# Linear attention on one Trainium2 core: the sums of the log decays made by a VectorE scan and spread by transfers, in place of TensorE products

## What is computed

```
q, k = elu(x @ Wq) + 1, elu(x @ Wk) + 1;  v = x @ Wv
a = sigmoid(x @ Wa + ba + 2.0)                    # one decay per token and head
S = a_t * S + k_t v_t^T;  z = a_t * z + k_t       # a recurrence over the tokens
out_t = (q_t S) / (q_t z + eps)
x1 = layernorm(x + out @ Wo)
```

## Time and profile before

| | us |
|---|---|
| three runs | 1453.0, 1449.99, 1451.87; median 1451.87 |
| the profiled execution, its own time | 1452.94 |
| its span, first to last instruction | 1450.9 |
| TensorE busy over the span | 1315.6 (91%) |
| ScalarE, VectorE, GpSimd busy over the span | 953.5, 833.1, 745.7 |
| the stage of the change | from the start to about 745 |

### The profile page before, as it was taken

The page is one execution under the profiler, slowest core; times in us unless marked ns, Lnnn a source line. Parts: engine busy times, 40 slices in busy tenths (PEclk is TensorE's granted clock), DMA queues, the critical chain, the costliest instruction groups (busy, mean ns, idle before and its releaser), DMA issues. The chain is left out here.

```text
span 1450.9 us, 31123 instructions
## 1 busy us (share of the span) xinstructions
PE 1315.6 (91%) x10437; PEld 1115.7 (77%) x10437; DVE 833.1 (57%) x1707; ACT 953.5 (66%) x2168; POOL 745.7 (51%) x841
## 2 busy tenths in 40 slices
PE   5899999999999999999988999982599999999780
PEld 4788888888888888888876777761488888888680
DVE  3345554445454455544556888857366666666564
ACT  4577767777777777777745777772466666656553
POOL 2244443444444444443547777740357777776753
PEclk9999999999999999999999999995599999999895
DMA  3300100001000100010023343422346666666737
GB/s 138 82 9 30 31 23 25 21 23 31 23 31 16 30 24 30 24 37 9 23 80 86 107 104 98 112 83 72 113 136 153 153 155 154 155 157 163 180 78 239
DMA packets 136851, 117.54 MB, mean 81 GB/s; under 512 B 46578, under 2 KB 121690, under 8 KB 136730
## 3 DMA queue, kind: packets, MB, share of 16 engines
q1 hardware_dynamic: 121754, 95.36, 21.6%
q0 software_dynamic: 14976, 20.62, 8.1%
HBM read 79.89 MB, written 33.58 MB: 78 GB/s over the span
## 5 line engine op out<-in xcount | busy, mean ns | idle before, releaser
L345 POOL TENSOR_SCALAR_AFFINE_SELECT a_decay<-a_decay 128x256 f32<-128x256 f32 x256 | 115.2, 454 | 258.2 <-ACT a_decay L433 256.7
L565 DVE TENSOR_TENSOR a_probs<-a_ps_s,a_decay 128x384 f32<-128x384 f32 x256 | 131.6, 552 | 158.5 <-PE a_ps_o L752 147.4
L354 POOL TENSOR_TENSOR a_key_sum<-a_probs 128x256 f32<-128x256 f32 x128 | 94.5, 738 | 169.9 <-DVE a_probs L565 157.9
L1877 POOL DMA_INDIRECT sum_rows<-e_y_out,e_target x78 | 125.8, 1613 | 81.0 <-ACT e_y_out L1931 56.5
L396 ACT ACTIVATE a_qk_exp<-a_ps_qk 128x512 f32<-128x512 f32 x128 | 76.5, 598 | 137.2 <-PE a_ps_qk L658 130.0
L658 PE MATMUL a_ps_qk<-a_xT_hi,a_w_hi 128*128 128x256 f32 x512 | 144.8, 283 | 3.6 <-ACT a_qk_relu L397 3.6
L658 PE MATMUL a_ps_qk<-a_xT_hi,a_w_lo 128*128 128x256 f32 x512 | 143.8, 281 | 0.0
L658 PE MATMUL a_ps_qk<-a_xT_lo,a_w_hi 128*128 128x256 f32 x512 | 143.7, 281 | 0.0
L558 DVE SCALAR_TENSOR_TENSOR a_qk<-a_qk_exp,a_qk_relu 128x512 f32<-128x512 f32 x128 | 89.1, 696 | 94.5 <-ACT a_qk_relu L397 94.3
L733 PE MATMUL a_ps_s<-a_qk 64*128 64x256 f32 (+1 forms) x1024 | 132.2, 338 | 0.6 <-DVE a_probs L565 0.5
L431 ACT ACTIVATE a_decay<-a_ps_c,a_c_now 128x256 f32<-128x256 f32 x256 | 124.4, 486 | 2.1 <-PE a_ps_c L723 1.2
(11 more groups left out here) (318 smaller groups left out, 4017.2 us busy)
## 6 DMA issues: line engine op xcount, KB each, us to landing
e_gu_raw<-in_L_ffn_gate_w SPq DMA_DIRECT2D x23, 512.0 KB
e_gu_raw<-in_L_ffn_up_w SPq DMA_DIRECT2D x23, 512.0 KB
e_dn_raw<-in_L_ffn_down_w SPq DMA_DIRECT2D x23, 512.0 KB, 5.3
a_x_in<-in_x SPq DMA_DIRECT2D x16, 256.0 KB, 2.7
a_x_res<-in_x SPq DMA_DIRECT2D x16, 256.0 KB
x_rows<-a_x SPq DMA_DIRECT2D x16, 256.0 KB, 2.2
x_bo_rows<-a_x_bo SPq DMA_DIRECT2D x16, 256.0 KB, 2.2
b_x_bo<-x_bo_rows SPq DMA_DIRECT2D x16, 256.0 KB, 2.9
```

Source lines behind the costliest of these rows:

```text
L345: pool.affine_select(out=d, in_=d, compare_op=ALU.is_ge, fill=0.0, base=0, pattern=[[0, 2], [1, P]], channel_multiplier=-1)\
L354: pool.tensor_tensor(key_sum[:], probs[:, :, P:N], probs[:, :, N:TRI], ALU.add).then_inc(keys_summed, 1)
L565: vec.tensor_tensor(probs[:, h, :], ps_s[h][:, 0:TRI], decay[h][:], ALU.mult)\
L1877: pool.indirect_dma_start(sum_dram, bass.IndirectOffsetOnAxis(target[par][:, blk:blk + 1], 0), y_out[par][:, blk, :], None, compute_op=ALU ...
```

## The change

VectorE sums -log(a) along the free axis with one scan, for 16 heads on 16 partitions (`sum_decay`, now VectorE's). TensorE turns only the result into the columns (`turn_c`, two transposes of the kind of the old `turn_dec`, after g = 5). SyncE stores the scan's result, 16 KB, to DRAM (`store_c`), and for each pair one transfer reads its two rows (2 KB) and writes them to all 128 partitions (`spread_c`, 256 KB), into a ring of four tiles in SBUF, three to four pairs ahead. `exp_decay` reads that tile. The columns have two buffers. z and the columns have a bank of their own, the one that ps_c had. Gone are the one-hot products, the triangle and its products, the three bf16 parts and their copies, `keep_cT` and `switch_c`. `log_decay` moves from g = 3 to g = 2, in the prologue from after pair 5 to after pair 2; SyncE's queue is written out, with no loop, and the loads of the next stage go out in three parts in the sequences 0, 1 and 2.

```diff
@@ TensorE
             def turn_x(b):
-                pe.wait_ge(cT_kept, b)
+                pe.wait_ge(v_done, VU * b)
             def project_z(b):
                 pe.wait_ge(x_lo_done, b + 1)
+                pe.wait_ge(c_kept, b)
...
-            def turn_dec(b):
-                pe.wait_ge(dec_done, b + 1)
-                pe.wait_ge(v_done, VU * (b + 1))
...
-            def sum_decay(b):
-                pe.wait_ge(dec_kept, b + 1)
-                pe.matmul(c_view[:, 0, :], upto[:], dec[:, 0, :], start=True, stop=True)
...
             def turn_c(b):
-                pe.wait_ge(c_split, b + 1)
...
+                pe.wait_ge(c_summed, b + 1)
+                for blk in range(NB):
+                    mm = pe.transpose(c_view[:, blk, :], cT[:, blk * P:(blk + 1) * P], ident[0:H, 0:H])
+                mm.then_inc(c_turned, 1)
             def project_v(b, half, blk):
                 if (half, blk) == (0, 0):
-                    pe.wait_ge(z_kept, b + 1)
+                    pe.wait_ge(x_lo_done, b + 1)
-            def spread_c(b, g):
-                pe.wait_ge(c_switched, 2 * b + 2)
-                pe.wait_ge(decay_exp[1], b * PAIRS + g)
-                for h in range(2):
-                    mm = pe.matmul(ps_c[:, h, :], pick_head[:, 2 * g + h, :], cT_now[:], start=True, stop=True)
-                mm.then_inc(c_spread, 1)
@@ SyncE
+            def store_c(b):
+                sp.wait_ge(c_summed, b + 1)
+                sp.dma_start(c_dram[b], cT[:]).then_inc(c_stored, 16)
+            def spread_c(b, g):
+                n = b * PAIRS + g
+                if g == 0:
+                    sp.wait_ge(c_stored, 16 * (b + 1))
+                if n >= ROWS_AHEAD:
+                    sp.wait_ge(decay_exp[1], n - ROWS_AHEAD + 1)
+                two_rows = c_dram[b, 2 * g:2 * g + 2, :].rearrange("(a h) n -> a (h n)", a=1)
+                sp.dma_start(c_rows[n % ROWS_AHEAD][:].rearrange("p h n -> p (h n)"), two_rows.to_broadcast([P, 2 * N]))\
+                    .then_inc(rows_loaded[n % ROWS_AHEAD], 16)
             def sequence(b):
-                load_x(b + 2)
-                load_residual(b)
-                store_x1(b - 1)
+                for g in range(PAIRS):
+                    ahead = b * PAIRS + g + ROWS_AHEAD - 1
+                    if g and ahead < B * PAIRS:
+                        spread_c(ahead // PAIRS, ahead % PAIRS)
+                    if g == 0:
+                        if b + 2 < B:
+                            load_x(b + 2)
+                        if ahead < B * PAIRS:
+                            spread_c(ahead // PAIRS, ahead % PAIRS)
+                    if g == 1 and b < cross.LOAD_PARTS:
+                        cross.load(sp, b)
+                    if g == 3 and b >= 1:
+                        load_residual(b)
+                    if g == 4 and b + 1 < B:
+                        store_c(b + 1)
+                    if g == 6 and b >= 1:
+                        store_x1(b - 1)
...
+            store_c(0)
+            for g in range(ROWS_AHEAD - 1):
+                spread_c(0, g)
@@ ScalarE
-            def exp_decay(b, g):
-                act.wait_ge(c_spread, b * PAIRS + g + 1)
+            def exp_decay(b, par, g):
+                n = b * PAIRS + g
+                rows, c_now = c_rows[n % ROWS_AHEAD], c_col[par]
+                act.wait_ge(c_kept, b + 1)
+                act.wait_ge(rows_loaded[n % ROWS_AHEAD], 16 * (n // ROWS_AHEAD + 1))
                 for h in range(2):
...
-                    act.activation(decay[h][:, 0:N], ps_c[:, h, :], ACT.Exp,
+                    act.activation(decay[h][:, 0:N], rows[:, h, :], ACT.Exp,
                                    bias=c_now[:, 0, head:head + 1], scale=-1.0)
...
-                        if g == PAIRS - 1:
-                            keep_cT(b + 1)
-                            switch_c(b + 1)
@@ VectorE
-            def keep_dec(b):
...
-            def split_c(b):
...
+            def sum_decay(b):
+                vec.wait_ge(dec_done, b + 1)
+                vec.wait_ge(c_turned, b)
+                vec.wait_ge(c_stored, 16 * b)
+                vec.tensor_tensor_scan(cT[:], scan_ones[:], decT[:], 0.0, ALU.mult, ALU.add).then_inc(c_summed, 1)
+            def keep_c(b, par):
+                vec.wait_ge(c_turned, b + 1)
+                if b >= 2:
+                    vec.wait_ge(decay_exp[1], (b - 1) * PAIRS)
+                vec.tensor_copy(c_col[par][:], c_view).then_inc(c_kept, 1)
...
-                    if g == 6 and has(b, 1):
-                        split_c(b + 1)
+                    if g == 4 and has(b, 1):
+                        sum_decay(b + 1)
+                    if g == 7 and has(b, 1):
+                        keep_c(b + 1, 1 - par)
```

More of the change, by code:

```diff
@@ L111, in keep, with load @@
         return act.copy(self.ctxT[:, :, first:first + rows], bank.rearrange("p (k n) -> p k n", k=KC)[:, :, 0:rows])
-    def load(self, sp):
+    def load(self, sp, part):
         ctx_in, mask, wq, bq, wk, bk, wv, bv, wo, bo, router_w = self.sources
@@ L149, in linear_attention @@
     VU = 2 * NB
-    CP = 3 * H
     TRI = N + P
+    ROWS_AHEAD = 4
     DECAY_SHIFT, EPS, Z_FLOOR = 2.0, 1e-6, -80.0
@@ L300, in _ @@
             load_x(1)
             load_residual(0)
-            load_x(2)
-            cross.load(sp)
-            with sp.Fori(1, B - 2) as b:
+            store_c(0)
+            for g in range(ROWS_AHEAD - 1):
+                spread_c(0, g)
+            for b in range(B):
                 sequence(b)
-            sp.wait_ge(x1_stored, 32)
-            sp.dma_start(cross.x_first[:], x1_rows[0]).then_inc(cross.first_loaded, 16)
-            for b in (B - 2, B - 1):
-                load_residual(b)
-                store_x1(b - 1)
@@ L318, in _ @@
                                pattern=[[-1, P]], channel_multiplier=1).then_inc(ident_ready, 1)
[L319 removed]
             pool.memset(ones[:], 1.0).then_inc(consts_step, 1)
[L321 removed]
+            pool.memset(scan_ones[:], 1.0).then_inc(consts_step, 1)
             pool.memset(eps_col[:], LN_EPS).then_inc(consts_step, 1)
[L323 to L336 removed]
+            pool.wait_ge(consts_step, 4)
             pool.memset(den_eps[:], EPS).then_inc(consts_ready, 1)
@@ L460, in sequence @@
                 for g in range(PAIRS):
-                    exp_decay(b, g)
-                    if g == 3 and has(b, 1):
+                    exp_decay(b, par, g)
+                    if g == 2 and has(b, 1):
                         log_decay(b + 1)
@@ L612, in sequence @@
                         finish_qk(*projected_before(b, g))
-                    if g == 5 and has(b, 1):
-                        keep_dec(b + 1)
                     weigh(b, g)
@@ L634, in _ @@
                     low_weights(2 + g)
-            keep_dec(0)
-            split_c(0)
+                if g == 2:
+                    sum_decay(0)
+                if g == 5:
+                    keep_c(0, 0)
             x_lo(1)
@@ L748, in weighted_values @@
                 for h in range(2):
-                    pe.matmul(out[h][:, 1, 0:P], ones[:, 0:DH], probs[:, h, 0:P], start=True, stop=True)
+                    pe.matmul(out[h][:, 1, 0:P], ones[:], probs[:, h, 0:P], start=True, stop=True)
                 pe.wait_ge(keys_summed, n + 1)
                 for h in range(2):
-                    mm = pe.matmul(out[h][:, 1, P:N], ones[:, 0:DH], key_sum[:, h, :], start=True, stop=True)
+                    mm = pe.matmul(out[h][:, 1, P:N], ones[:], key_sum[:, h, :], start=True, stop=True)
                 mm.then_inc(o_made, 1)
@@ L782, in sequence @@
                             project_v(b + 1, g - 1, 1)
-                        if g == 4:
-                            turn_dec(b + 1)
                         if g == 5:
-                            sum_decay(b + 1)
-                        if g == 6:
                             turn_c(b + 1)
@@ L802, in _ @@
                     project_v(0, (g - 1) // NB, (g - 1) % NB)
-                if g == VU + 2:
-                    turn_dec(0)
-            sum_decay(0)
-            turn_c(0)
+                if g == VU:
+                    turn_c(0)
             turn_x(1)
```

129 lines of the change are left out of this document (40 added, 89 removed).

## The result

The changed kernel takes 1420.57 us, the median of four runs from 1418.74 to 1424.65, against 1451.86 for the kernel before: a ratio of 0.9782, with a 95% interval of 0.977 to 0.9795. That is 31.3 us less; 1423 was forecast, with a range of 1408 to 1438. The profiled execution took 1418.74 with a span of 1416.9, so the traces differ by 34.0 us of span. It is the quickest of its four runs, and the one of before is 1.07 us above its median; that is why the traces differ by more than the medians.

The account below looks back on a forecast made before the run. TensorE, busy throughout the stage's middle, was taken as the bound. Spread 14.4, small products 11.8 and prologue 3.0 made 29.2 us off 1452.94, so 1423.7, or 1422.7 against the median, given as 1423; range 1408 to 1438.

Parts of the forecast that it names:

- Nothing for the spread: Rival, TensorE: the scores' exposed first weight load takes up the 0.12 us; only small products and prologue pay, 1437, chance 0.10.
- The whole spread counts: Rival, TensorE ahead of the scores: 0.23 us a pair gained, 1409.5 us, or 1397.5 with the gap; chance 0.15.
- half of the spread was hidden already: Step, TensorE: the spread ran beside the second head's scores, so removing it gains 0.12 us a pair, not 0.23.
- takes 3.8 us at the granted clock of 0.51: Step, prologue: 18 products from the projection's start at about 45.0 to the second pair, starting near 48.9 instead of 52.66.
- -5: Prologue's end case: if the clock no longer falls, the weighing of pair 0 sets the start; -5 us against -3.0 taken.
- still in time: Step, VectorE's weighing: it moves about 0.12 us forward and the second head's mask is ready for it.
- if it were late, the 1.3 us would hide it: Step, VectorE's weighing: a mask late by 0.1 or 0.2 us is covered before TensorE asks for the weighing.
- At 72 GB/s a spread is 3.6 us: Step, transfers: rate taken from the bias broadcasts; eight spreads and four plain transfers are 32.7 of 42.3 us.
- the queue three quarters full: Step, transfers: a sequence's spreads and plain transfers, 32.7 us, fit into its 42.3 us.
- transfers set the pace: Rival, DMA: under 52 GB/s slower than now; at 40 GB/s about 1657 us, ScalarE waiting on DMA; chance 0.05.
- busy 4.00 of 4.00: Sign in the earlier trace: TensorE's busy time beside 303 GB/s of loads, read as its products not slowing.
- Another engine next: Rival: the score, values and weighing ring or ScalarE would be over 1 us longer, gain vanishes, 1451; chance 0.03.

Follow-up runs that it names:

- experiment 4: Changed kernel with five products shaped like the removed small ones put back in pairs 4 and 5 of fifteen sequences: 1435.94 us, 0.9877 of the kernel before.
- experiment 1: Changed kernel with two products of 48 rows and 256 columns put back ahead of the scores, pairs 2 to 5 of fifteen sequences: 1427.42 us, 0.9819.
- 2: Changed kernel with two products of all 128 rows and 256 columns ahead of the scores, pairs 2 to 5 of fifteen sequences: 1438.62 us, 0.9891.
- Experiment 11: Changed kernel with one 48-row product ahead of the scores in pairs 2 and 3, one in each half of the rows in 4 and 5: 1427.02 us, 0.9805.
- Experiment 7: Changed kernel with the chain for c(0) (log decay, sum, copy, turn) moved back to the prologue's end: 1432.37 us, 0.984 of the kernel before.
- experiment 3: Changed kernel with only the first four spreading transfers issued, all later pairs reading those four tiles: 1422.85 us, 0.9784 of the kernel before.
- experiment 5: Changed kernel with each spreading transfer followed by three more broadcasts of the same rows into unread DRAM: 1544.78 us, 1.0596 of the kernel before.
- experiment 10: Changed kernel with later spreads replaced by two 128 KB broadcasts a pair of the same 1 KB bias row, results unused: 1422.92 us.
- 8: Changed kernel with one value projection of pairs 1 and 2 moved to just ahead of the q and k projection, its copy likewise: 1416.63 us, 0.973.
- 6: Changed kernel with each pair's spread as two transfers of 1 KB rows in place of one of 2 KB: 1425.77 us, 0.9784 of the kernel before.

## Why the prediction was right, and where it was not

**The sum.** Forecast 29.2 us off; 30.8 at the last sequence's start and 31.3 in the medians. The forecast's 14.4 + 11.8 for the fifteen periods is 26.2, and the trace has 2.74 + 14 x 1.68 = 26.3. But the first period's 2.74 holds 1.06 that belong to the prologue, whose last products now run at the high clock; on that reckoning the periods gave 15 x 1.68 = 25.2 and the prologue 5.65. With the small products at the 0.83 us a sequence of experiment 4, the terms are 12.7 us for the spreads (forecast 14.4), 12.5 for the small products (11.8) and 5.65 for the prologue (3.0). That the sum came within 1.6 us is in part luck: one term was too large and two too small.

**The spread: the size was right, the reason wrong.** 0.12 us a pair, from comparing whole groups in the earlier trace rows, is what the trace after shows (0.85 for 0.97) and what experiment 1 gives back (0.11). Over a whole pair it is a little less: the pitch fell by 0.11, 0.08, 0.05, 0.13 and 0.12 us in the pairs 0 to 3 and 7, which had no small product, since in the pairs 1 and 2 the products behind the scores take 0.04 and 0.07 us longer than before; no run shows why. The bounds of nothing and of 0.23 fell, and with them two rivals. "Nothing for the spread" was right that the scores' first weight load is exposed, and wrong on what it costs: the bare group of the earlier trace rows holds that load already, so nothing comes off the 0.12. "The whole spread counts" is refuted by 1, where two products put back cost 0.11 a pair and not 0.23 (2 shows what the whole would look like). The step that failed is "half of the spread was hidden already", beside the second head's scores. Experiment 11 shows that one product hides whole, and that one in each half does too, which leaves nothing to hide beside. What they fill is time that is lost anyway. At the scores, about 0.1 us passes ahead of the first product and about 0.1 behind it. The first product of the scores is followed by the next of its own head after 0.32 us in the changed kernel, and after 0.22 in experiment 1, where it isn't the first any more. The two products of the spread stood in the rows of one head, took 0.22 us one after the other, and filled that tenth, so 0.12 were left.

What the second tenth is, the trace after suggests: the weights of the first product of a new shape are loaded with the product itself and not ahead of it (289.86 and 289.86 above; 289.55 for 289.65 where the shape stays). It fits that the weighted values, whose weights are 64 columns wide (a load takes 136 ns and not 186), lose only half as much: their first product is followed after 0.27 us where 0.22 is usual. No run tests this reading by itself.

The Trainium skill, "TensorEngine Tiling (Array Packing)", Key Properties, says that a change of mode drains the engine. The trace agrees on the gap ahead (0.21 where 0.11 is usual), and the prediction used it for that alone. The second tenth, behind the first product, is what the runs add. "TensorE: Matmul & The Clock Gate", Part 3, says that products in different row groups run together: that holds too (278.13 and 278.13 in experiment 11), but it isn't where the 0.12 came from. What it says besides, and the prediction repeats, that a weight load overlaps running products only then, does not agree with this trace: the load at 289.55 runs beside a product on the same 128 rows that started at 289.54.

**The small products.** Forecast 0.79 us a sequence; the changed kernel shows 0.72 if the spread is taken at 0.12, and experiment 4 0.83. The difference is what the pairs 1 and 2 fell short of 0.12. Both lie within the 1 us in all that the prediction allowed each way (0.07 x 15), and the earlier trace rows priced the two groups within 0.01.

**The prologue: undersized.** Forecast -3.0, measured -5.65 at the second pair. The mechanism and the times up to the first projection were right: log decay done at 30.34 (near 31 forecast), scan 0.68 us, the first exponentials of the decays at 43.85 (44.2), the first projection at 44.75 (45.0). The step that failed is "takes 3.8 us at the granted clock of 0.51". TensorE was busy for 4.15 of the 6.00 us before 46, the clock did not fall, and the 18 products took 2.3 us. Even before they took 3.53 (49.13 to 52.66), as the last of them ran at the high clock again. Of the 5.65 us, 4.38 are the earlier start of the projection (49.13 to 44.75) and 1.27 the quicker products. The prediction's own end for that case, -5, was nearest, though the second pair follows the last product by the usual 0.21 us and not, as said there, the weighing of pair 0, done at 46.72. Experiment 7 puts the late chain back and gets the low clock with it. I had taken the fall from a window behind a hole that the change itself closed.

**Costed at nothing.** VectorE's scan: right, as TensorE stays busy. ScalarE's reads: 506 ns for 486, within the 0.05 us of the bound; with the two of 128 columns (395 for 385) that is 0.06 us a pair, hidden by its wait for TensorE. The mask: "still in time" was wrong, since it now comes last 52 times, for 0.6 us in the mean; "if it were late, the 1.3 us would hide it" was right. SyncE's queue: right, since experiment 3, which drops nearly all spreads, gains nothing.

**The transfers: far too dear.** The step "At 72 GB/s a spread is 3.6 us", with "the queue three quarters full", failed. The share is 0.25, and 0.09 without the spreads (experiment 3): 0.16 of 42.4 us for eight spreads is 0.85 us each. The estimate from it, 77 / 0.25 = 308 GB/s at full share, is near the plain loads of the earlier trace rows (303 at 0.94); at the share of 0.83 of experiment 5, with its writes to DRAM, only 195 GB/s were moved. The landing of 3.1 us is mostly not occupation, since a spread occupies the queues for 0.85. The worst case that the prediction drew up for 128 reads of one row did not come: 4.1 us to land for the very same row (experiment 10). The rival "transfers set the pace" got its 0.05 from that mis-sized rate. Experiment 5 shows that late rows do stop all, as it said, but there SyncE's issues and waits were as full as the queue. And "busy 4.00 of 4.00" could not show that TensorE's products are not slowed by transfers; experiment 3, with the same period at 0.09 as at 0.25, does so for that much traffic.

**Another engine next.** It did not come: with 0.46 us a sequence more taken away in 8, TensorE's period still shrank by all of it, so the next bound is at least that far off.

## What to carry to other kernels

Where one engine is busy throughout, compare whole groups from first start to the next group's first start, with and without the part in question; the duration or pitch of the part alone would have said twice the gain. On TensorE count a change of shape as work, about 0.2 us for each into products with 64 or 128 rows and 128 columns of weights, and put products of one shape together: that was worth 0.46 us a sequence here, over half of what all the small products cost. When a change closes a hole on TensorE, don't carry the low clock behind that hole over to the new kernel. And when transfers are added, count what SyncE has to issue and to wait for in order, beside the bytes.

## What the runs showed that I had not expected

- A change of TensorE's shape costs twice: about 0.1 us ahead of the first product and about 0.1 us behind it (0.05 into 64 columns), and a product in either half of the rows fits into the second for 0.01 to 0.02 us (experiments 8, 11). It is not so for every change: from 128 rows by 128 columns to 128 by 16 the products go on at 0.11 us (46.12 to 46.23 in the trace after).
- A broadcast of 2 KB of DRAM to 128 partitions occupies the queues no longer than plain loads would: a share of 0.25 at 77 GB/s, 3.1 us to land. Reading the very same 1 KB each time costs somewhat more, 0.38 for 0.27 and 4.1 us for 3.0 (experiments 6, 10).
- With a share of 0.83 in the mean the same transfer lands in 8.7 us, an issue takes SyncE 1.08 us instead of 0.36, and the kernel takes 1.0596 times the time of before (experiment 5).
- A scan over 16 partitions x 256 takes 0.68 us (30.37 in the trace after), as long as one over 128 x 256.
- An ACTIVATE of 128 x 256 takes 506 ns from SBUF, with or without transfers beside it, and took 486 from PSUM (experiment 3).
